# Layer 4: the projections of half 1 behind tiles 0 and 1, mixing ahead of the next tile's scores, unread products left out, the last tiles reordered

## What is computed

```
xn = layernorm(x) * gamma + beta
q_lat, k_lat, v_lat = xn @ Wq.T, xn @ Wk.T, xn @ Wv.T
q, v = per-head products of q_lat with Qc, of v_lat with Vc
alpha = sigmoid(xn @ Wa_w.T + Wa_b)            # per row, head and key channel
kn = k_lat / max(|k_lat|, 1e-12)
for each row t:  S = alpha_t * S + kn_t (x) v_t ;  o_t = q_t . S     # S starts at 0 in each batch
out = o @ Wo.T + x          (the program then takes layernorm(x + out))
```

## Time and profile before

| | us |
|---|---|
| median of 3 runs | 642.63 (640.96 to 642.87) |
| span of the profiled execution | 622.9 |
| the layer of the change in that span | 323.5 to 445.2 |
| the profiled execution's own time | not recorded beside its span |

### The profile page before, as it was taken

How to read it: one execution, slowest core, us unless ns; L and a number is a source line. 1 busy time by engine, 2 the same in 40 slices (tenths; PEclk the granted TensorE clock), 3 DMA queues, 4 the chain that set the end, 5 groups by cost and what they waited for, 6 DMA issues and landing times. The chain is left out here.

```text
span 622.9 us, 12073 instructions
## 1 busy us (share of the span) xinstructions
PE 485.7 (78%) x4162; PEld 365.7 (59%) x4162; DVE 443.2 (71%) x1475; ACT 276.2 (44%) x679; POOL 244.2 (39%) x283
## 2 busy tenths in 40 slices
PE   3798548776789587798997868978679879779990
PEld 1466415535639466677865557766357755369980
DVE  4699799889748846756775889994478648327746
ACT  4599912211231344455124636652346512247732
POOL 3732893547514103555010523230255233616640
PEclk9979856688779786899999967988979898969985
DMA  7300030500000035316000000000281400151121
GB/s 228 117 2 2 1 135 8 166 1 1 1 1 1 1 98 106 68 27 113 2 0 1 2 0 2 1 3 0 99 363 42 102 1 19 54 144 49 44 91 50
DMA packets 27998, 33.38 MB, mean 54 GB/s; under 512 B 4961, under 2 KB 21073, under 8 KB 27426
## 3 DMA queue, kind: packets, MB, share of 16 engines
q1 hardware_dynamic: 26002, 29.13, 16.0%
q0 software_dynamic: 1504, 3.15, 1.5%
q10 hardware_dynamic: 432, 0.33, 0.2%
HBM read 26.44 MB, written 6.16 MB: 52 GB/s over the span
## 5 line engine op out<-in xcount | busy, mean ns | idle before, releaser
L2076 POOL TENSOR_TENSOR ea_scaled_rows<-ea_scaled_rows 128x768 f32<-128x768 f32 (+2 forms) x21 | 24.0, 1144 | 50.9 <-ACT ea_scaled_rows L1990 49.8
L3526 POOL DMA_INDIRECT em_results<-em_y_slot,slot_rows x31 | 29.7, 959 | 28.8 <-DVE em_y_slot L3653 27.9
L277 ACT ACTIVATE norm_log<-norm_var 128x4 f32<-128x4 f32 x20 | 4.1, 207 | 78.4 <-DVE norm_var L262 78.3
L3397 PE MATMUL banks<-em_slotT,em_weights 128*128 128x128 f32 x248 | 34.9, 287 | 2.7 <-ACT em_weights L3289 2.7
L3644 DVE SCALAR_TENSOR_TENSOR em_innerT<-banks,em_bias_of,em_soft 128x128 f32<-128x128 f32 x62 | 19.0, 346 | 23.7 <-ACT em_soft L3468 20.9
L3397 PEld LDWEIGHTS banks<-em_slotT,em_weights 128*128 128x128 f32 x248 | 32.0, 202 | 3.5 <-issue 3.5
L38 PE MATMUL banks<-ea_w_high,ea_x_high 128*128 128x384 f32 x64 | 27.1, 424 | 8.8 <-DVE ea_acc L2167 8.5
L2677 POOL TENSOR_TENSOR ga_to_end<-ga_cum 128x512 f32<-128x512 f32 x8 | 8.8, 1096 | 60.0 <-DVE ga_to_mid L2739 60.0
L1990 ACT ACTIVATE ea_scaled_rows<-banks,ea_gate 128x192 f32<-128x192 f32 x64 | 23.3, 417 | 19.0 <-PE banks L38 18.7
L3064 POOL TENSOR_TENSOR ca_prob<-ca_prob,ca_most 128x1232 f32<-128x1232 f32 x8 | 18.0, 2250 | 18.5 <-DVE ca_most L3117 18.5
L3468 ACT ACTIVATE em_soft<-banks,em_bias_of 128x128 f32<-128x128 f32 x62 | 19.4, 364 | 12.5 <-PE banks L3397 12.2
(11 more groups left out here) (509 smaller groups left out, 1540.9 us busy)
## 6 DMA issues: line engine op xcount, KB each, us to landing
em_up<-in_em_up SPq DMA_DIRECT2D x3, 1536.0 KB, 10.8
ea_wide<-ea_gates SPq DMA_DIRECT2D x4, 1024.0 KB, 11.8
em_down<-in_em_down SPq DMA_DIRECT2D x3, 768.0 KB, 12.2
em_slots<-slot_rows SPq DMA_DIRECT2D x1, 2108.0 KB, 9.8
w_qkv<-in_w_qkv SPq DMA_DIRECT2D x1, 1536.0 KB, 7.3
slot_rows<-em_slots SPq DMA_DIRECT2D x1, 1360.0 KB, 8.5
cos_half<-in_cos_half SPq DMA_DIRECT2D x1, 1024.0 KB, 8.2
sin_half<-in_sin_half SPq DMA_DIRECT2D x1, 1024.0 KB, 10.4
```

The costliest lines, as they stand in the source:

```text
L2076: step(pool.tensor_tensor(scaled_rows[:, k, 0:n], scaled_rows[:, k, 0:n], scaled_rows[:, k, n:2 * n], ALU.add))
L3397: ins = pe.matmul(s.ps[:, k * P:(k + 1) * P], weights[:, n % NW, k // 2, k % 2 * P:(k % 2 + 1) * P], slotT[:, n], start=True, stop=True, s ...
L3526: pool.indirect_dma_start(core.results[:, :], bass.IndirectOffsetOnAxis(ap=slot_rows[:, s, P:P + 1].bitcast(U32), axis=0), y_slot[:, s % N ...
```

## The change

TensorE's new order splits `front` into `decay` (z) and `read` (q), and the projections into `rows_T`, `key`, `query`, `value`, which become stages of the order; half 1's key, query and value come behind tile 0's scores. In each tile `back(g)` (mixing) now stands ahead of `mid(g + 1)` (scores), and the last tiles are woven together. `kt` is left out of the plan for tiles 3 and 7.

```diff
-            out = [("front", 0), ("front", 1), ("size", 0), ("size", 1), ("front", 2), ("mid", 0)]
-            for g in range(NT):
-                out += [("front", g + 3)] if g + 3 < NT else []
-                out += [("last", g - 1)] if g >= 1 else []
-                out += [("mid", g + 1)] if g + 1 < NT else []
-                out += [("back", g)]
-            return out + [("last", NT - 1)]
+            out = [("rows_T", 0), ("decay", 0), ("key", 0), ("query", 0), ("decay", 1), ("read", 0), ("size", 0),
+                   ("read", 1), ("value", 0), ("rows_T", 1), ("decay", 2), ("read", 2), ("mid", 0), ("key", 1),
+                   ("query", 1), ("value", 1), ("decay", 3), ("read", 3)]
+            for g in range(HT + 1):
+                out += [("back", g)]
+                out += [("size", 1)] if g == 0 else []
+                out += [("mid", g + 1)]
+                out += [("decay", g + 4), ("read", g + 4)] if g + 4 < NT else []
+                out += [("last", g)]
+            g = HT + 1
+            return out + [("back", g), ("mid", g + 1), ("back", g + 1), ("mid", g + 2), ("last", g), ("last", g + 1),
+                          ("back", g + 2), ("last", g + 2)]
...
+        def products_before(g):
+            return 10 * g - (g + HT - 1) // HT - g // HT
+        def scaled_keys(g):
+            return products_before(g) + 9
```

```diff
-                for g in range(2):
-                    front(g)
-                    move_q(g)
-                for g in range(2):
-                    log(g)
-                for b in range(B):
-                    roots(b)
-                for g in range(2):
-                    decays(g)
+                rows_T(0)
+                core.norm.act(act, step)
+                front(0)
+                key(0)
+                log(0)
+                query(0)
+                front(1)
+                move_q(0)
+                decays(0)
+                log(1)
+                roots(0)
+                scales(0)
+                rows_T(1)
+                move_q(1)
+                decays(1)
+                value(0)
+                scales(1)
                 front(2)
+                log(2)
                 move_q(2)
-                log(2)
                 mid(0)
+                key(1)
+                query(1)
+                value(1)
                 for g in range(NT):
                     if g + 2 < NT:
                         decays(g + 2)
                     if g + 3 < NT:
                         front(g + 3)
+                    if g + 2 < NT:
+                        scales(g + 2)
+                    if g == HT + 2:
+                        core.norm.act(act, step)
+                    back(g)
+                    if g + 3 < NT:
+                        move_q(g + 3)
                         log(g + 3)
-                        move_q(g + 3)
-                    if g + 1 < NT:
+                    if g + 1 < NT and not ends(g + 1):
                         mid(g + 1)
-                    back(g)
-                    if g in (HT + 1, NT - 1):
-                        core.norm.act(act, step)
+                    if not ends(g):
+                        carry(g)
+                    if g == 1:
+                        roots(1)
+                core.norm.act(act, step)
```

```diff
-                for g in range(2):
-                    cap(g)
-                scan(0)
-                for b in range(B):
-                    size(b)
-                scan(1)
-                for b in range(B):
-                    unit(b)
-                decay(0)
-                cap(2)
-                decay_all(0)
-                decay(1)
-                decay_all(1)
-                mid(0)
-                scan(2)
+                core.norm.dve(dve, step, x[:, half(0)], xn[:, half(0)])
+                step.wait()
+                scaled(0)
+                core.norm.dve(dve, step, x[:, half(1)], xn[:, half(1)])
+                cap(0)
+                square(0)
+                scan(0)
+                size(0)
+                cap(1)
+                step.wait()
+                scaled(1)
+                scan(1)
+                unit(0)
+                decay(0)
+                decay(1)
+                scan(2)
+                square(1)
+                mid(0)
+                decay_all(1)
                 for g in range(NT):
                     if g + 2 < NT:
                         decay(g + 2)
+                    if g >= 1:
+                        last(g - 1)
+                    if not ends(g):
+                        back(g)
                     if g + 3 < NT:
                         scan(g + 3)
-                    back(g)
+                    if g == 0:
+                        size(1)
                     if g + 1 < NT:
                         mid(g + 1)
-                    if g + 2 < NT:
+                    if g + 2 < NT and not begins(g + 2):
                         decay_all(g + 2)
-                    if g >= 1:
-                        last(g - 1)
-                    if g == NT - 1:
-                        last(g)
-                    if g in (HT + 1, NT - 1):
-                        hb = half(g // (NT - 1))
-                        core.norm.dve(dve, step, res[:, hb], out[:, hb])
+                    if g == 1:
+                        unit(1)
+                    if g == HT + 1:
+                        core.norm.dve(dve, step, res[:, half(0)], out[:, half(0)])
+                last(NT - 1)
+                core.norm.dve(dve, step, res[:, half(1)], out[:, half(1)])
```

More of the change, by code:

```diff
@@ L2418, in _, with query @@
                     ins.then_inc(s.filled, 1)
-                    s.taken(pe)
-                    s = ring[f"ql{b}"]
+                def query(b):
+                    ring[f"xT_{b}"].taken(pe)
+                    s = ring[f"ql_{b}"]
                     s.claim(pe)
@@ L2423, in _, with key, value @@
                               stop=True).then_inc(s.filled, 1)
-                    s = ring[f"k{b}"]
+                def key(b):
+                    ring[f"xT_{b}"].taken(pe)
+                    s = ring[f"k_{b}"]
                     s.claim(pe)
                     pe.matmul(s.ps[:, :], t["ga_wkk"][:, :], xT[:, half(b)], start=True, stop=True).then_inc(s.filled, 1)
-                    s = ring[f"vr{b}"]
+                def value(b):
+                    ring[f"xT_{b}"].taken(pe)
+                    s = ring[f"vr_{b}"]
                     s.claim(pe)
@@ L2440, in size, with decay @@
                               stop=True).then_inc(s.filled, 1)
-                def front(g):
+                def decay(g):
+                    ring[f"xT_{g // HT}"].taken(pe)
                     s = ring[f"z_{g}"]
@@ L2449, in front, with read @@
                     ins.then_inc(s.filled, 1)
-                    ring[f"ql{g // HT}"].taken(pe)
+                def read(g):
+                    ring[f"ql_{g // HT}"].taken(pe)
                     s = ring[f"q_{g}"]
@@ L2529, in last @@
                     ins.then_inc(s.filled, 1)
-                stages = {"size": size, "front": front, "mid": mid, "back": back, "last": last}
+                stages = {"rows_T": rows_T, "key": key, "query": query, "value": value, "size": size, "decay": decay,
+                          "read": read, "mid": mid, "back": back, "last": last}
                 for stage, g in order():
@@ L2610, in mid @@
                     s.ready(act)
-                    if g >= 2 and (g - 2) % HT < HT - 1:
+                    if g >= 2 and not ends(g - 2):
                         ring[f"st_{g - 2}"].ready(act)
@@ L2695, in _, with scaled @@
                 core.wait_loaded(dve, "ga")
-                for b in range(B):
+                def scaled(b):
                     hb = half(b)
-                    core.norm.dve(dve, step, x[:, hb], xn[:, hb])
-                    step.wait()
                     step(dve.tensor_tensor(xn[:, hb], xn[:, hb], spread(rows["gamma"], 1, [P, HT, P]), ALU.mult))
@@ L2702, in _, with square @@
                                       ALU.add).then_inc(xn_ready, 1)
-                for b in range(B):
+                def square(b):
                     hb = half(b)
-                    ring[f"k{b}"].taken(dve)
+                    ring[f"k_{b}"].taken(dve)
                     dve.tensor_tensor(k_square[:, hb], kT[:, hb], kT[:, hb], ALU.mult).then_inc(square_ready, 1)
```

89 lines of the change are left out of this document (49 added, 40 removed).

## The result

| us | before | after |
|---|---|---|
| median of 4 runs | 642.75 (640.96 to 647.38) | 623.38 (616.97 to 633.65) |
| ratio of the undisturbed runs | | 0.9695, interval 0.9639 to 0.9752 |
| profiled execution, its span | not recorded, 622.9 | 624.2, 622.4 |
| the layer of the change | 121.7 | 102.6 |

The account below looks back on a forecast made before the run. VectorE bounds the layer's middle, with TensorE near; head and tail are chains of waits. Gains 8.8 + 2.2 + 0.7 + 7.0 = 18.7 us, less 0.7 for the clock: 642.6 - 18.0 = 624.6 us, range 621.0 to 632.5.

Parts of the forecast that it names:

- Around the span: Outside the profiled span: 19.7 us, taken as median 642.6 less span 622.9, which the change does not touch.
- Head: Layer start to tile 0's first product, 27.6 us before: half 0 going early lets it come sooner, gain 8.8 us.
- Fill: Tile 0's first product to tile 2's, 16.1 us before: VectorE's work then takes 13.9 us, gain 2.2 us.
- Middle: Tile 2's first product to tile 7's, 48.6 us before: intervals sum to 47.5, total gain 0.7 us after the scale's price.
- its 0.4: Middle: price of GpSimd's block scales coming late, 0 to 4.2 us possible over six tiles, 0.4 us taken.
- Tail: Tile 7's first product to the next layer, 29.4 us before: new sum 22.4 us, gain 7.0 us.
- Three lonely rounds become two: Tail: rounds of about 10, 10 and 6 us, each tile alone through the engines, become two; tail gain 7.0 us.
- My one VectorE wait over 3 us: Tail: sign of a right forecast, only one VectorE wait longer than 3 us there in the new trace.
- The clock fall in the tail: Tail: part of a fall of TensorE's clock, 0.7 us deducted, bounds 0 and about 3 us.
- A: Middle: half clock at tile 0 or 1 with VectorE waiting on TensorE, loses 6.5 to 7 us; 631 to 632; chance 0.14.
- C: Whole filled pipeline at 1.2 GHz: 7.5 us more per tile, slower from three tiles, 654 us at four; chance 0.03.
- B: Scale late by 0.7 us in six tiles (4.2), tail gives back 2 to 3; gain 12, 630 us; chance 0.15.

Follow-up runs that it names:

- kept warm: Discarded TensorE products added ahead of mixing in tiles 0 and 3 to 6, against the changed kernel with three further reorderings; ratio 0.9656 to the kernel before.

## Why the prediction was right, and where it was not

The time, 623.4, lies 1.2 us under the forecast of 624.6, and the mechanism of the forecast is in the main the one that ran: VectorE filled where it had been idle. How near the total came is in part luck: the four runs lie between 617.0 and 633.7 us, one kernel's layer moved by 3.0 us between two executions, and the errors below partly cancel. By steps:

- **Around the span.** Wrong. I took 19.7 us around the span; every run with both numbers has 1.8 to 2.0 (624.2 and 622.4 in the kernel after). The trace of before belonged to an execution of about 624.7 us, with a short last layer (114.3). The term was on both sides of the sum, so it did no harm.
- **Head.** Right, 8.67 for 8.8. The rows' copy came 6.4 us into the layer (ScalarE, 335.23) where it had been at 7.4, tile 0's first product at 18.9 where I had 18.8. With the early half undone, 8.75 of it went.
- **Fill.** Right, 2.32 for 2.2, and with the unread `q_all` back 0.59 of it went. The warming products had cover as I said, more of it than they needed: without them nothing changed there.
- **Middle.** Mis-sized, 1.88 for 0.7: it took 46.70 us where I had 47.9. Of my five intervals (9.9, 9.65, 9.05, 9.4, 9.5, without a wait) measured were 9.49, 9.58, 8.87, 9.26 and 9.50, the last two with a wait for the scale inside. Without these waits each is shorter than I had counted, by 1.9 us in sum. The scale cost more than its 0.4: 0.68 and 0.39 at tiles 5 and 6, and 0.39 at tile 7, which belongs to the tail. The chain that I priced it from, the row at 404.32, is tile 6's and not tile 5's. For the order of mixing and scores I had nothing, and in the new queues TensorE indeed kept VectorE waiting nowhere in the middle; but I followed the bank claims of the new order only, and not what the old order would do in this kernel, which is 3.1 us. The unread products were well priced at 0.6 to 0.7 each (0.6 seen); what I did not have is the clock fall that came with them.
- **Tail.** The number near (6.20 for 7.0 less 0.7), by luck, and its cause wrong. The clock was full in this tail (1.00), so the 0.7 was not spent; 22.4 us by my sum, which comes out only with ScalarE's 0.9 in it, were 23.24, with tile 7's late scale in them. "Three lonely rounds become two" is not what shortened it: the weaving costs 2.3 us, and the tail of before becomes as short by VectorE adding the residual before its scan instead of at the end of the round, which empties the bank that the next scores wait for. In the kernel before TensorE began 2.42 us late at that point, at the moment when VectorE had done. The prediction has no term for it: I had not asked who held the bank. My one VectorE wait over 3 us is there (3.76), and the 2.1 for last 5 was 2.15: the timing of the new order was right step by step, and the comparison with the old one was not.
- **The clock fall in the tail.** Bounds about right: nothing in the tail of one execution of the kernel after, 3.1 us in that of another, where I had 0 to about 3 and took 0.7.

**The rivals.** A and C had the lower clock in the middle. It came there once, late (0.57 at 400:404 in the kernel after), and cost nothing: the middle took 46.70 us with it and 46.69 in the second execution, where the clock held until 404. B had the scale late at six tiles, 4.2 us, and a tail that gives back a wait: seen were three tiles and 1.46 us, and the tail kept its gain. The rule of the Trainium skill ("GPSIMD Engine Reference", section "1. Specifications", on the interfaces that GpSimd shares with VectorE) pointed the right way: more chains were late than I had taken, and in the three late ones GpSimd's second small copy took 0.66 to 0.68 us, in those of tiles 2 and 3 it took 0.19. The long end for all six did not come. The rule of the Trainium skill on short idles ("TensorE: Matmul & The Clock Gate", section "A second HAM failure mode: psum-queue depth-cycling") agrees with the falls ahead of the tail and in it (0.50 at 406:410 in one execution), and it does not say in which executions they come.

What stays open: why the last layer takes 112 us in one group of runs and up to 131 in others, and what the profile's "remote" is; what the unread products cost when the clock holds (some 2.1 us by the estimate above, but not run); and how the 3.1 us of mixing ahead of the scores divide between the banks and the order of work.

## What to carry to other kernels

Where banks go round in the order of a list, moving an entry changes who waits for whom: ask of each claim who held the bank, in the old order as in the new one, and look at a TensorE gap labelled "issue" beside the VectorE instruction that ended just before it. Undo each part of a change alone before believing a sum that came out right: here an order that I had priced at nothing was worth 3.1 us, and one that I had counted as a gain cost 2.3, and the total, within 1.2 us, showed neither. Compare a layer between the same two instructions, not spans, while another layer moves by 15 us on its own.

## What the runs showed of the hardware

- One kernel's layer repeats to 0.02 us in three of its stretches, while its tail takes 23.24 or 26.30 us by where the granted clock falls. In the first case it fell at 400:404 and was hidden, in the second at 406:410 (0.50) and was not. The first, by windows and in TensorE's timeline of the kernel after:

```profile
396.00:400.00 4.00, 2.16 (x15) 1.18 (x13) 3.97 (x8) 3.01 (x8) 2.81 (x5) 1.00 0.02 6
400.00:404.00 4.00, 4.00 (x70) 3.53 (x68) 3.58 (x13) 2.05 (x5) 1.11 (x3) 0.57 0.00 0
```
```profile
400.61 2.08 PE L2497 MATMUL banks<-ga_q_mid,ga_k_mid 64*128 64x128 f32 x16
```

- It fell with TensorE at work for 1.95 of the 4 us before in one case and for 2.16 in the other, and did not fall with TensorE busy 7.92 of 8 (kept warm). But in the kernel after it also stayed up behind this stretch:

```profile
386.00:390.00 4.00, 2.41 (x18) 1.98 (x20) 3.93 (x6) 2.48 (x6) 1.62 (x3) 1.00 0.00 0
```

- Lower clock need not cost time: 0.52 from 362 to 372 with both halves first, and 9.57 us from tile 2 to tile 3 for 9.49; with the unread products back, as much of it or more in the same interval went with 1.0 and 1.7 us.
- The last layer, unchanged in all kernels, took 111.8 to 131.1 us, and went with the group in which a kernel ran, each on its own chip, and with waits on "remote" (none in the five executions under 115 us).
